# Masked attention sublayers: where VectorE adds the mask to the next scores, and where ScalarE copies the next values

## The chip, the cores and the metric

One NeuronCore of one Trainium2 chip runs the whole program; there is no other core and no collective. The metric is the device time of one execution in microseconds. Before the change it is 3198.39 us, the median of three runs.

## The reference

A decoder of four layers runs on 8 sequences of 100 tokens with 256 features. Each layer is a self-attention, a cross-attention over 361 context rows and a feed-forward part, each on a layer-normed input and added to the stream. Three of the four self-attentions mask their scores, have 16 heads, and are the subject here:

```python
# L0: Q is x itself (16 per head), K = x Wk + bk, V = x Wv + bv (64 per head)
scores = jnp.einsum('bhqd,bhkd->bhqk', Q, K) + mask          # causal
o = jnp.einsum('bhqk,bhkd->bhqd', softmax(scores), V)
return x + gelu(o, approximate=False) @ Wf + bf
# L2: causal, V of 16 per head, no Gelu;  L3: rotary q and k, a window of |i - j| <= 32
```

The fourth (L1) has one head, no mask and a transposed output. The softmax maximum of every query row and head is taken over the masked scores.

## The kernel before, in words

The program has three stages with one instruction stream per engine each (`stream`, written by hand): A, B and C. A stage is a list of items; an item is one sequence of one sublayer. `KINDS` gives the order: A = first (8 items), whole, mixture, turned, cross; B = causal (8), wide; C = band (8), cross. "first" is the masked attention of layer 0 (all heads, with the Gelu), "causal" that of layer 2, "band" that of layer 3. I number the items of each masked sublayer 0 to 7. Between the stages lie feed-forward parts, and behind C a recurrent loop that is most of the time.

An item's step of the loop has four rounds, r = 0 to 3, and in one step of the loop an engine works on several items at once: with item i in the middle, the scores are made for i+1 and the weighted values and the output product for i-1 or i-2. Each engine runs its list strictly in order and waits on semaphores. For the masked kinds the pieces are:

- TensorE makes the scores of item i+1 as rows of queries in PSUM banks 0 to 3 (`score_round`, L748 or L736), in round 0, right after the first of the two key tiles of item i.
- VectorE adds the mask to those rows (L1858, 100 x 1600 elements), waits for itself, and takes the negated maxima (L1860). That is `tops_of`. The maxima free the score banks.
- TensorE turns the maxima (`turn_tops`, L777, at the end of round 3), and VectorE adds them to the queries (`lower`, L1880), so that the second score product comes out with the maximum subtracted.
- TensorE makes the second score product of item i in two key tiles, transposed, in banks 4 and 5 (`key_rows`, L813 or L804), one tile in round 0 and one in round 1. The two tiles use the same banks, so tile 1 waits until ScalarE has taken tile 0.
- VectorE adds the transposed mask to each tile (`mask_rows`, L1888), ScalarE takes its exponential (L1491).
- TensorE multiplies with the values (`weighted_half` L827 and L834 for "first"), VectorE divides by the sum (`divided_half`, last operation L1904; `divided` L1920 for the other kinds), TensorE makes the output product (`out_product`, L905 and L907), VectorE adds it to the stream (`add_out`, L1928).
- For "first", ScalarE takes eight Gelus of 128 x 100 in place (L1590), four per half of the heads, and the output product in round 0 of the next step waits for all eight. TensorE makes the item's own values in two halves (`own_values`, L720, rounds 2 and 3). ScalarE copies half 0 out of PSUM (L1395, round 2), VectorE half 1 (L1979, round 3).
- `group_work` makes what serves four sequences at once: it turns the normed rows (L597) and projects queries and keys (L606), with the copies out of PSUM on ScalarE (L1395) or, for "band", rotations on VectorE (L1829, L1831).

Everything that TensorE writes outside the score and tile banks goes through banks 6 and 7 in turn (`open_m`): a product can start only when the product two before it has been copied out. This ties TensorE's order to ScalarE's and VectorE's order. With item i in the middle, VectorE's order in rounds 0 and 1 for "first" is: output of i-2, division of half 0 of i-1, mask of tile 0, division of half 1, mask of tile 1, mask of the next scores, maxima. For "causal" and "band" there is one division ahead of tile 0 and none between the tiles.

Items with group work in their loop step: first 0, 1, 2 and 6; causal and band 1, 2, 5 and 6. The others I call light.

Of the kernel before, what the change touches and what calls it, by code (L numbers as in the profile page):

```python
# [21 lines left out]
ALU = mybir.AluOpType  # L22
# [128 lines left out]
def build(nc, dram, out):  # L151
    with ExitStack() as ctx:
# [43 lines left out]
        def cst(name):  # L196
            at, n = CONST[name]
            return const[:, at:at + n]
# [243 lines left out]
        def kind_of(ph, i):  # L442

            return KINDS[ph][i // B] if 0 <= i < B * len(KINDS[ph]) else None
# [928 lines left out]
        def _(act):  # L1373
# [103 lines left out]
            def own_values(ph, i, half):  # L1477

                if kind_of(ph, i) == "first":
                    evacuate(mem[ph]["vA"][0:S, i % 2, 512 * half:512 * half + 512], S, 512, ph, "v", i, half)  # L1480
                else:
                    evacuate(v1[0:S, i % 2, 0, :], S, D, ph, "v", i, half)
# [50 lines left out]
            def stream(ph):  # L1533

                nc.scalar.preload_act_table(ACT.Exp)
                for i in range(-3, items_of(ph) + 2):
# [8 lines left out]
                    for r in range(4):  # L1545
# [36 lines left out]
                        if then == "cross" and ph == "C" and r in (1, 2):  # L1582
                            values_of(ph, i + 1, r - 1)
                        group_work(ph, i, r)
                        if past == "first" and r in (1, 2):
                            half = r - 1
                            act.wait_ge(sem["divided"], 2 * (i - 1) + half + 1)
                            for c in range(4 * half, 4 * half + 4):
                                o_ = mem[ph]["oT"][:, columns_of(c)]
                                last = nc.scalar.activation(o_, o_, ACT.Gelu, bias=abv[:, c:c + 1])  # L1590
                            last.then_inc(sem["gelu"], 1)
                        if then in ("first", "turned") and r == 2:
                            own_values(ph, i + 1, 0)
                        if ph == "B":
                            wide_step(ph, i, r, 0)
                            wide_step(ph, i, r, 1)
# [93 lines left out]
        def _(dve):  # L1690
# [142 lines left out]
            def group_work(ph, i, r):  # L1833

                for s, kind in enumerate(KINDS[ph]):
                    for g in range(2):
# [5 lines left out]
                        if kind == "mixture" and (at_, r) == (0, 3):  # L1842
# [5 lines left out]
                            top_two(4, small[:, 0, 0:4, :], small[:, 1, 0:4, :], gates4[:, g, :, 0:E],  # L1848
                                    lambda last: last.then_inc(sem["gates_ready"], 1))

            def tops_of(ph, i, c):

                kind, tops = kind_of(ph, i), mem[ph]["tops"]
                dve.wait_ge(sem["sc_full"], before(ROUNDS, ph, i, c + 1))
                if kind in ("first", "band", "causal"):
                    rows = banks[0:S, 0:4, 0:4 * S].rearrange("p j (c k) -> p j c k", c=4)
                    over = cst("window" if kind == "band" else "causal")[0:S, :].unsqueeze(1).unsqueeze(1).to_broadcast([S, 4, 4, S])
                    step(nc.vector.tensor_tensor(rows, rows, over, ALU.add))  # L1858
                    dst = tops.rearrange("p c (j e) -> p j c e", j=4)[:, :, :, 16]
                    nc.vector.tensor_reduce(dst, rows, AX, ALU.max, negate=True).then_inc(sem["sc_free"], 1)  # L1860
                elif kind == "cross":
                    nc.vector.tensor_reduce(tops[:, c, 16:P:32], banks[0:S, 0:4, 0:NK], AX, ALU.max, negate=True  # L1862
                                            ).then_inc(sem["sc_free"], 1)
                else:
                    keys = NK if kind == "whole" else S
                    nc.vector.tensor_reduce(peak[:, i % 2:i % 2 + 1], banks[0:S, 0, 0:keys], AX, ALU.max, negate=True
                                            ).then_inc(sem["peaks"], 1)
# [142 lines left out]
            def stream(ph):  # L2010

                for i in range(-3, items_of(ph) + 2):
# [6 lines left out]
                    for r in range(4):  # L2019
# [10 lines left out]
                            mask_rows(ph, i, 0)  # L2030
                        if past == "first" and r == 0:
                            divided_half(ph, i - 1, 1)
                        masked_late = now in ("first", "band", "causal") and then in ("first", "band", "causal")
                        if then not in (None, "mixture", "wide") and (r == 0 or then == "cross") and not masked_late:
                            tops_of(ph, i + 1, r)
                        if now in ("first", "band", "causal") and r == 1:
# [1108 lines left out]
```

## Time and profile before

| | |
|---|---|
| median of 3 runs | 3198.39 us (3196.77 to 3203.35) |
| the profiled execution | 3194.56 us |
| its span in the trace | 3192.7 us |
| mean granted TensorE clock | 0.961 of full speed |
| TensorE matmul, VectorE, ScalarE busy | 2961.0, 1556.2, 744.0 us |
| first, causal, band sublayers in the trace | about 29 to 223, 897 to 1009, 1565 to 1684 us |

A time in the timeline is the distance from the span's start. The number in brackets at the end of a row is how long the engine had been idle before that instruction, and what released it. A row without brackets followed directly on the one before. The 2.85 us by which the span is shorter than the execution's own time lie outside the records.

### The profile page before, as it was taken

How to read it: one execution, taken by the hardware profiler on the slowest of the kernel's cores; microseconds unless marked ns; L12 is line 12 of the kernel's file. 1: busy time of each engine (PE TensorE's matmuls, PEld its weight loads, DVE VectorE, ACT ScalarE, POOL GpSimd, SP SyncE). 2: the span in 40 equal slices, each digit the busy share in tenths (PEclk: the TensorE clock that was granted, in tenths of full speed). 3: DMA queues.
4: the chain of work that ended last, by engine and by line, in shares of the span. 5: the costliest groups of instructions: out<-in, count | busy, mean ns of one | idle time of the engine just before them, and what ended most of it. 6: DMA issues, size and time to landing. Idle time of an engine off the chain costs nothing.

```text
span 3192.7 us, 63820 instructions
## 1 busy us (share of the span) xinstructions
PE 2961.0 (93%) x25719; PEld 1664.5 (52%) x25719; DVE 1556.2 (49%) x4141; ACT 744.0 (23%) x1837; POOL 280.7 (9%) x673
## 2 busy tenths in 40 slices
PE   6888889899978999999889999999999999999897
PEld 4554456589755555555546643434444444444386
DVE  4545335411256566300575532466666666666643
ACT  2331123311122455211014411111111111111111
POOL 2112211020311010000311100000000000000011
PEclk9999989999989999999889999999999999999999
DMA  4000000189330000411000156000000000000176
GB/s 148 1 1 1 10 26 15 34 303 326 119 120 1 1 1 1 143 53 66 1 1 3 32 163 176 12 23 24 23 25 20 23 24 24 20 23 24 40 267 228
DMA packets 81363, 202.99 MB, mean 64 GB/s; under 512 B 32894, under 2 KB 56107, under 8 KB 68484
## 3 DMA queue, kind: packets, MB, share of 16 engines
q1 hardware_dynamic: 77208, 192.76, 18.4%
q0 software_dynamic: 3968, 7.56, 0.7%
q8 instruction: 140, 2.29, 0.3%
q14 instruction: 47, 0.39, 0.0%
HBM read 170.06 MB, written 37.53 MB: 65 GB/s over the span
## 4 chain that ended last, share of the span: by engine, by line
PE 79%; DVE 10%; DMA 4%; ACT 3%; issue 2%; POOL 1%; SPq 1%; DVEq 0%; POOLq 0%; ACTq 0%
PE banks L1273 32%; PE banks L1087 7%; PE banks L905 4%; PE banks L606 4%; PE banks L798 2%; PE banks L1151 2%; PE banks L1163 2%; PE banks L927 2%; PE banks L1242 2%; PE banks L559 2%; PE banks L945 1%; PE banks L951 1%; PE banks L967 1%; PE banks L693 1%; PE banks L1320 1%
## 5 line engine op out<-in xcount | busy, mean ns | idle before, releaser
L1273 PE MATMUL banks<-arena 128*32 128x384 f32 x12800 | 1034.3, 486 | 1.9 <-DVE arena L2276 1.1
L1273 PEld LDWEIGHTS banks<-arena 128*32 128x32 f32 x12800 | 416.6, 110 | 613.7 <-issue 610.0
L1663 ACT ACTIVATE arena<-arena 128x256 f32<-128x256 f32 x200 | 83.2, 416 | 759.4 <-DVE arena L2288 759.4
L2288 DVE TENSOR_TENSOR arena<-banks,arena 128x256 f32<-128x256 f32 x200 | 84.9, 425 | 199.8 <-PE banks L1273 198.7
L1087 PE MATMUL banks<-arena 128*128 128x400 f32 x512 | 172.5, 499 | 1.5 <-DVE arena L2239 0.8
L606 PE MATMUL banks<-XNT,arena 128*128 128x400 f32 x384 | 153.2, 542 | 9.7 <-ACT XNT L1395 3.7
L905 PE MATMUL banks<-arena 128*100 128x256 f32 x512 | 139.2, 426 | 14.7 <-ACT arena L1590 5.1
L1384 ACT ACTIVATE arena<-banks 128x512 f32<-128x512 f32 (+2 forms) x103 | 59.2, 575 | 341.8 <-PE banks L1151 137.4
L1087 PEld LDWEIGHTS banks<-arena 128*128 128x128 f32 x512 | 97.1, 190 | 76.8 <-DVE arena L2239 1.4
L1862 DVE TENSOR_REDUCE arena<-banks 100x4 f32<-100x1444 f32 x64 | 106.3, 1661 | 62.8 <-PE banks L754 62.6
L2579 POOL TENSOR_TENSOR rstd<-rstd 100x3 f32<-100x3 f32 (+1 forms) x120 | 23.1, 193 | 1239.5 <-DVE rstd L1817 1233.1
L798 PEld LDWEIGHTS banks<-arena 32*121 32x121 f32 x1536 | 100.6, 187 | 58.5 <-ACT arena L1497 35.7
L1497 ACT ACTIVATE arena<-banks 121x600 f32<-121x600 f32 x128 | 85.8, 670 | 184.4 <-PE banks L798 184.4
L1395 ACT ACTIVATE arena<-banks 128x361 f32<-128x361 f32 (+4 forms) x147 | 72.0, 490 | 233.4 <-PE banks L951 103.0
L2670 POOL DMA_INDIRECT region_rows<-arena x20 | 18.4, 920 | 1226.5 <-DVE arena L2417 1223.4
L905 PEld LDWEIGHTS banks<-arena 128*100 128x100 f32 x512 | 91.7, 186 | 52.2 <-ACT arena L1590 5.9
L798 PE MATMUL banks<-arena 32*121 32x100 f32 x1536 | 112.5, 278 | 6.2 <-ACT arena L1497 6.2
L1087 PE MATMUL banks<-XNT,arena 128*128 128x400 f32 x288 | 101.6, 513 | 11.5 <-DMA arena<-gu 10.5
L606 PEld LDWEIGHTS banks<-XNT,arena 128*128 128x128 f32 x384 | 75.9, 205 | 69.5 <-issue 15.0
L559 PE MATMUL banks<-arena 128*100 128x256 f32 x448 | 100.0, 385 | 5.5 <-DVE X L2162 2.9
L2292 DVE TENSOR_TENSOR arena<-arena,banks 128x128 f32<-128x128 f32 x200 | 57.6, 288 | 96.4 <-ACT arena L1663 96.4
L1928 DVE TENSOR_TENSOR X<-X,banks 100x256 f32<-100x256 f32 x56 | 23.5, 420 | 161.6 <-PE banks L907 101.4
(385 smaller groups left out, 4276.7 us busy)
## 6 DMA issues: line engine op xcount, KB each, us to landing
arena<-fc SPq DMA_DIRECT2D x22, 1024.0 KB, 6.8
arena<-pj SPq DMA_DIRECT2D x22, 1024.0 KB, 5.2
arena<-gu SPq DMA_DIRECT2D x21, 1024.0 KB, 7.1
arena<-whh SPq DMA_DIRECT2D x32, 384.0 KB, 10.8
arena<-dn SPq DMA_DIRECT2D x21, 512.0 KB, 5.3
arena<-xw SPq DMA_DIRECT2D x400, 24.0 KB
xw<-arena SPq DMA_DIRECT2D x6, 1536.0 KB, 7.2
arena<-hh SPq DMA_DIRECT2D x16, 512.0 KB, 3.2
```

The lines of the kernel that those rows point to most:

```text
L559: last = nc.tensor.matmul(u[0:S, 0:cols], a, b, start=i == 0, stop=bias is None and i == len(parts) - 1)
L606: last = nc.tensor.matmul(u[:, 0:4 * S], w[:, kk], XNT[:, kk, columns_of(4 * g, 4)], start=kk == 0, stop=kk == C - 1)
L798: last = nc.tensor.matmul(banks[0:KR, 4 + jj, columns_of(kc)], m["kX"][r, i % 3, c, key_chunk(kc)], qA[r, c, columns_of(b)], start=True, s ...
L905: last = nc.tensor.matmul(u[0:S, 0:D], o_, w_, start=c == 0, stop=bias is None and c == len(parts) - 1)
L927: last = nc.tensor.matmul(u[0:S, 0:cols], XNT[:, kk, columns_of(b)], wa("f_w", C)[:, kk, 512 * j:512 * j + cols], start=kk == 0, stop=j < ...
L1087: last = nc.tensor.matmul(u[:, 0:HALF], w, x[:, half * HALF:(half + 1) * HALF], start=i == 0, stop=i == len(parts) - 1)
L1273: last = nc.tensor.matmul(banks[32 * j:32 * j + 32, 2 * c + i, 0:384].rearrange("p (g n) -> p g n", g=3), hT[:, 1 - i, 32 * ub:32 * ub + 3 ...
L1395: nc.scalar.activation(dst, u[0:rows, 0:cols], func, bias=bias, scale=scale).then_inc(sem[evac_], 1)
L1497: nc.scalar.activation(dst, banks[0:KR, 4:6, 0:KC * S], ACT.Exp).then_inc(sem["t_free"], 1)
L1663: nc.scalar.activation(rz[:, c, :], pre[:, c, :], ACT.Sigmoid).then_inc(sem["rz_done"], 1)
L1862: nc.vector.tensor_reduce(tops[:, c, 16:P:32], banks[0:S, 0:4, 0:NK], AX, ALU.max, negate=True).then_inc(sem["sc_free"], 1)
L2288: nc.vector.tensor_tensor(pre[:, c, :].rearrange("p (g n) -> p g n", g=2), banks[:, 2 * c + i, 0:2 * P].rearrange("p (g n) -> p g n", g=2) ...
```

## The change

It has two parts. On VectorE `tops_of` is cut in two for the masked kinds: the mask on the next scores becomes `mask_scores`, called in round 0 after the mask of key tile 0 (for "first" after the division of half 1 as well), and the maxima stay where they were, behind the mask of tile 1. On ScalarE, for "first", the eight Gelus go together into round 2, and the copy of the next item's value half 0 is put ahead of them. No operation is added or removed.

```diff
                         group_work(ph, i, r)
-                        if past == "first" and r in (1, 2):
-                            half = r - 1
-                            act.wait_ge(sem["divided"], 2 * (i - 1) + half + 1)
-                            for c in range(4 * half, 4 * half + 4):
+                        if then in ("first", "turned") and r == 2:
+                            own_values(ph, i + 1, 0)
+                        if past == "first" and r == 2:
+                            act.wait_ge(sem["divided"], 2 * i)
+                            for c in range(8):
                                 o_ = mem[ph]["oT"][:, columns_of(c)]
                                 last = nc.scalar.activation(o_, o_, ACT.Gelu, bias=abv[:, c:c + 1])
-                            last.then_inc(sem["gelu"], 1)
-                        if then in ("first", "turned") and r == 2:
-                            own_values(ph, i + 1, 0)
+                            last.then_inc(sem["gelu"], 2)
...
+            def mask_scores(ph, i):
+
+                dve.wait_ge(sem["sc_full"], before(ROUNDS, ph, i, 1))
+                rows = banks[0:S, 0:4, 0:4 * S].rearrange("p j (c k) -> p j c k", c=4)
+                over = cst("window" if kind_of(ph, i) == "band" else "causal")[0:S, :].unsqueeze(1).unsqueeze(1).to_broadcast([S, 4, 4, S])
+                step(nc.vector.tensor_tensor(rows, rows, over, ALU.add))
+
             def tops_of(ph, i, c):
 
                 kind, tops = kind_of(ph, i), mem[ph]["tops"]
-                dve.wait_ge(sem["sc_full"], before(ROUNDS, ph, i, c + 1))
+                if kind not in ("first", "band", "causal"):
+                    dve.wait_ge(sem["sc_full"], before(ROUNDS, ph, i, c + 1))
                 if kind in ("first", "band", "causal"):
                     rows = banks[0:S, 0:4, 0:4 * S].rearrange("p j (c k) -> p j c k", c=4)
-                    over = cst("window" if kind == "band" else "causal")[0:S, :].unsqueeze(1).unsqueeze(1).to_broadcast([S, 4, 4, S])
-                    step(nc.vector.tensor_tensor(rows, rows, over, ALU.add))
...
                         if past == "first" and r == 0:
                             divided_half(ph, i - 1, 1)
-                        masked_late = now in ("first", "band", "causal") and then in ("first", "band", "causal")
+                        masked = then in ("first", "band", "causal")
+                        masked_late = now in ("first", "band", "causal") and masked
+                        if masked and r == 0:
+                            mask_scores(ph, i + 1)
                         if then not in (None, "mixture", "wide") and (r == 0 or then == "cross") and not masked_late:
                             tops_of(ph, i + 1, r)
```

## Rows read from the trace of the kernel before

**Rows 1.** The page's chain that ended last, shares by engine.
```profile
PE 79%; DVE 10%; DMA 4%; ACT 3%; issue 2%; POOL 1%; SPq 1%; DVEq 0%; POOLq 0%; ACTq 0%
```
**Rows 2.** Lines L1858, L1860 and L1590: durations in ns (min/median/max), first and last start.
```profile
L1858 DVE TENSOR_TENSOR banks<-banks,const_sb x24: 1822/1823/1833, 29.5 to 1664.9; 100x1600 f32<-100x1600 f32 x24
L1860 DVE TENSOR_REDUCE arena<-banks x24: 1825/1826/1827, 31.4 to 1666.8; 100x16 f32<-100x1600 f32 x24
L1590 ACT ACTIVATE arena<-arena x64: 361/363/378, 61.6 to 218.6; 128x100 f32<-128x100 f32 x64
L1590 ACT ACT_TABLE_LOAD  x8: 1283/1283/1283, 60.3 to 215.0; - x8
```
**Rows 3.** Timeline of first, item 3, rounds 1 to next 0: start us, us, engine, line.
```profile
107.72 0.95 PE L813 MATMUL banks<-arena 32*100 32x100 f32 x16 [0.27 <-ACT arena L1491]
109.07 0.57 DVE L1904 TENSOR_TENSOR arena<-banks,arena 128x400 f32<-128x400 f32 x1
109.68 0.99 DVE L1888 TENSOR_TENSOR banks<-banks,causalT 100x800 f32<-100x800 f32 x1
110.71 0.84 ACT L1491 ACTIVATE arena<-banks 100x800 f32<-100x800 f32 x1 [3.04 <-DVE banks L1888]
111.57 1.28 ACT L1590 ACT_TABLE_LOAD   x1
112.86 2.26 ACT L1590 ACTIVATE arena<-arena 128x100 f32<-128x100 f32 x8
115.02 0.58 ACT L1395 ACTIVATE arena<-banks 100x512 f32<-100x512 f32 x1
115.74 0.53 PE L777 MATMUL banks<-const_sb,arena 100*128 100x100 f32 x4 [2.37 <-ACT arena L1395]
116.11 3.62 PE L905 MATMUL banks<-arena 128*100 128x256 f32 x16
```
**Rows 4.** Timeline of first, item 1, rounds 2 and 3.
```profile
66.62 0.60 ACT L1395 ACTIVATE arena<-banks 100x512 f32<-100x512 f32 x1
69.11 1.88 PE L720 MATMUL banks<-arena,XNT 128*100 128x512 f32 x4
70.83 0.51 PE L777 MATMUL banks<-const_sb,arena 100*128 100x100 f32 x4
```
**Rows 5.** Timeline of first, item 6, rounds 2 and 3.
```profile
174.86 0.60 ACT L1395 ACTIVATE arena<-banks 100x512 f32<-100x512 f32 x1
177.72 0.51 PE L777 MATMUL banks<-const_sb,arena 100*128 100x100 f32 x4
```
**Rows 6.** Timeline of first, item 7: the second key product, the output product.
```profile
193.59 0.87 PE L693 MATMUL banks<-arena 128*128 128x361 f32 x2 [1.06 <-ACT arena L1395]
197.60 6.60 PE L905 MATMUL banks<-arena 128*100 128x256 f32 x16 [2.71 <-ACT arena L1590]
```
**Rows 7.** Timeline of causal, item 3, rounds 0 to 2.
```profile
944.53 0.99 DVE L1888 TENSOR_TENSOR banks<-banks,causalT 100x800 f32<-100x800 f32 x1
947.33 3.49 PE L905 MATMUL banks<-arena 128*100 128x256 f32 x8
947.44 1.00 DVE L1888 TENSOR_TENSOR banks<-banks,causalT 100x800 f32<-100x800 f32 x1 [1.92 <-PE banks L813]
950.21 1.83 DVE L1860 TENSOR_REDUCE arena<-banks 100x16 f32<-100x1600 f32 x1
951.95 0.41 DVE L1928 TENSOR_TENSOR X<-X,banks 100x256 f32<-100x256 f32 x1
```
**Rows 8.** Timeline of band, items 3 and 4: TensorE.
```profile
1625.59 1.97 PE L905 MATMUL banks<-arena 128*100 128x256 f32 x8
1630.35 0.93 PE L777 MATMUL banks<-const_sb,arena 100*128 100x100 f32 x4 [2.79 <-DVE arena L1860]
1638.40 3.74 PE L905 MATMUL banks<-arena 128*100 128x256 f32 x8
```
**Rows 9.** Windows: length; PE, PEld, DVE, ACT, POOL busy (count); granted clock; DMA.
```profile
1632.00:1645.00 13.00, 10.85 (x68) 5.41 (x60) 9.61 (x16) 1.67 (x2) 6.13 (x16) 0.50 0.01 2
```

## The prediction

> **What bounds the kernel now.** I read the chain of waits first: TensorE holds 79% of it and VectorE 10% [rows 1]. The recurrent loop and the feed-forward parts make up most of the TensorE share, and the change doesn't touch them. Then I read the timeline of the three masked sublayers, since a sum over the program says nothing about an edit of order. There no engine is full: TensorE, VectorE and ScalarE hand work to each other, and one item's loop step is as long as the longest ring of waits. So the question for each of the items is which instruction ends the ring, and whether the moved work stands ahead of it.
>
> The moved VectorE instruction takes 1.82 us and stands 24 times in the program; three of these (ahead of item 0 of each sublayer, where nothing masked is in the middle) keep their place, so 21 move [rows 2]. One place on VectorE costs 1.86 us, the 1.82 and a short wait for itself. Its maxima (1.83 us) stay.
>
> **Part one, causal and band (14 moves).** Between the masks of the two key tiles VectorE idles: 1.92 us with TensorE at full clock [rows 7], since the exponential and the second tile must come between. The next scores are ready by then, as TensorE makes them right behind tile 0. The moved mask starts 0.9 us after the start of the tile 0 mask (that is how closely masks follow one another) and is through 2.77 us after it; the tile 1 mask starts 2.91 us after it now (947.44 less 944.53). It fits, with 0.14 us to spare, and with more where the clock is half. So the maxima come 1.86 us sooner in all 14, and what that is worth depends on what comes next:
> - Where only the maxima are waited for, all 1.86 us. In band item 3 TensorE's turning of the maxima sat idle for 2.79 us behind them, and its output product had ended long before, at 1627.56 [rows 8]. Causal item 0 and band items 0 and 3 are so: 3 x 1.86 = 5.6.
> - Where the output product ends shortly before the maxima, the gain stops there. In causal item 3 VectorE adds the output at 951.95, right behind the maxima, but the product ends at 947.33 + 3.49 = 950.82 [rows 7]: 1.95 less 0.88, so 1.07. I work causal 4 and band 4 (its L905 ran 3.74 us from 1638.40 [rows 8]) in the same way: 0.82 and 0.83. Sum 2.7.
> - In band item 2 the rotations stand between the tiles. The mask goes in front of them and pushes the tile 1 mask 0.97 us back, and the maxima gain the rest, 0.88. In causal 2 and 6 TensorE is nearly full with projections and waited only 0.38 us on this: 0.8 for both. Sum 1.6.
> - In causal 1 and 5 and band 1, 5 and 6 the copy of the turned rows or TensorE's own work ends the ring: 0.
> The bounds: no gain at all, and 14 x 1.86 = 26. I take 5.6 + 2.7 + 1.6 = 9.9 us gained.
>
> **Part two, first (7 moves, and all the Gelus).** Here VectorE isn't idle between the tiles, because the division of half 1 stands there. In item 3 its last operation starts at 109.07 and the tile 1 mask follows at 109.68 without a wait, though TensorE had that tile ready at 107.72 + 0.95 = 108.67 [rows 3]. So the moved mask pushes the tile 1 mask, and ScalarE's exponential behind it, back by 1.86 us, while the maxima end where they did. Queued behind that exponential on ScalarE are the copies of round 1, the table load and the Gelus.
> - Light items 3, 4, 5. Now: exponential 110.71, table load, eight Gelus to 115.12, value copy 115.02, then the turning of the maxima at 115.74 (it waited 2.37 us for the copy's bank), then the output product at 116.11 [rows 3]. After: exponential 112.57, copy 113.30 to 113.90, load 1.29, Gelus 2.26 to 117.45, output product 117.5. The turning moves forward to 114.35, but the output product is ahead of everything of the next round 0 in TensorE's queue and now waits for the Gelus. Loss 1.4 each, 4.1 for three. The stall behind the copy goes; the Gelus are late next.
> - Item 1. The value copy stood at 66.62 [rows 4]; after: 68.48 to 69.08. Four Gelus used to be behind the exponential and four between copies; now load 1.28 and eight Gelus (2.26) follow and end at 72.6, and the copy of the third key projection (0.60) only then frees the bank for value half 1. That product starts at 73.2 instead of 69.11, and the turning, 1.72 us behind it, at 74.9 instead of 70.83 [rows 4]. Loss 4.1.
> - Item 6 has the same order with a query projection: 174.86 + 1.86 + 0.60 + 1.28 + 2.26 + 0.60 = 181.5 for the turning instead of 177.72 [rows 5]; the output product used to start 1.0 us behind it and now 0.4. Loss 3.1.
> - Item 2. TensorE reaches tile 1 late there and the moved mask is covered, but a query copy falls behind the Gelus: 0.3.
> - Items 7 and 8 (8 is the step in which the last Gelus are taken). No mask moves. The first four Gelus and the load ran while TensorE made the keys; now the load starts only behind the second key copy, whose product ends at 193.59 + 0.87 = 194.46: 194.46 + 0.58 + 1.28 + 2.26 = 198.6, while now the last Gelu ends and the output product starts at 197.60 [rows 6]. Loss 1.0 each, 2.0.
> - Item 0: TensorE is full, 0.
> Bounds: 8 us if TensorE's own stream hides half of items 1 and 6, 25 us if each lengthened gap also costs clock (below). I take 4.1 + 4.1 + 3.1 + 0.3 + 2.0 = 13.6 us lost. The table loads stay at 8 [rows 2].
>
> **Sum.** 13.6 - 9.9 = +3.7 us. Against the profiled execution, 3194.56 (span 3192.7 and 1.9 around it), that is 3198.3. That execution is 3.8 below the median of the runs, 3198.39, so I forecast 3202.1 for the median.
>
> **The clock.** TensorE's output product of 16 matmul passes took 3.62 us in item 3 and 6.60 in item 7 behind a 2.71 us gap [rows 3, 6], so a gap of this size can leave it at 1.2 GHz for 2.98 us more; the 2.37 us gap in item 3 did not. After the change the gap ahead of that product is 2.6 us in the light items. The Trainium skill ("TensorE: Matmul & The Clock Gate", section "Why this matters for your kernels") asks that no long idle gaps stand between bursts, because the array falls back to half clock; it speaks against the change in "first" and for it in causal and band. Item 7 agrees with it; item 3 shows that its gap was still short enough.
>
> **The rivals.**
> - Clock lost in first (chance 0.25). Three of the seven lengthened gaps (items 1 and 3 to 8) leave the output product at half clock: 3 x 2.98 = 8.9, so 3202.1 + 8.9 = 3211. For it: item 7. Against it: item 3 at a gap 0.3 us shorter.
> - Clock won in causal and band, the other side (0.15). In band item 4 the granted clock was 0.50, that is 1.2 GHz [rows 9]. Its output product, now what ends the ring, takes 3.74 us against 1.97 in item 3 [rows 8], and the turning 0.93 against 0.51 [rows 4, 8]. The tile 1 product takes 0.7 more as well, by the 2.63 us that VectorE idled ahead of some tile 1 masks against the 1.92 of [rows 7]. If shorter gaps keep the clock at 2.4 GHz, that is 2.9 per item. It decides from four such items on: 11.6, so 3202.1 - 11.6 = 3190.5. Against it: VectorE and ScalarE still take most of the ring, so gaps remain.
> - The moves don't count (0.10). The causal and band gains and the first losses are both taken up by what stands next in TensorE's order: 3198. For it: heavy items give 0 already.
> - My sum as it stands: 0.50.
>
> **How the numbers follow.** A measurement of this kernel can tell about 0.2% (6.4 us) from no change, so "same" is 3192.0 to 3204.8. The forecast case lies in it with about three quarters of its weight, since 2.7 us more are enough to leave it (0.38 same, 0.12 slower); the third rival lies in it wholly, and 0.02 of each clock case. Slower: 0.12 + 0.23 = 0.35. Faster: 0.13. Same: 0.38 + 0.10 + 0.04 = 0.52. The range: 3192 to 3212 leaves out most of the second rival and little of the first.
>
> **What would show it.** In the changed profile: in causal and band the next scores' mask starts 0.9 us behind the tile 0 mask, the tile 1 mask keeps its 2.9 us distance, and causal and band are 4.5 and 5.4 us shorter. In first the idle ahead of the tile 1 mask is nil and its distance from the division 1.86 us larger; the turning of the maxima waits for them and no longer for the copy; the output product waits for the Gelus; the step of items 3 to 5 grows from 18.4 to 19.8 us, and the last Gelu comes 12 to 14 us later. I am wrong if the light items of first don't grow, if the tile 1 mask of causal slips by more than 0.2 us, or if the clock in rows like [rows 9] moves by tenths.

## The result, and the profile after

The changed kernel took 3213.9 us in the median of 5 executions (3202.66 to 3223.18) against 3201.47 for the kernel before on the same chip (3196.77 to 3203.48): a ratio of 1.0042, 95% interval 1.0025 to 1.006. Timed once more on another chip it was 1.0056 (1.0027 to 1.0085). So the change makes the kernel slower by 12 to 15 us. I had forecast 3202.1, with 3192 to 3212 as the range: the sign of the sum was right, the time lay 1.9 us above the range, and "same", to which I had given the most weight (0.52), was not it.

The profiled execution of the changed kernel took 3204.47 us (span 3202.7), and its span is 10.0 us longer than that of before. (Time less span is 1.8 us here and was 1.9 before, 3194.56 less 3192.7; the 2.85 us given ahead of the prediction is wrong.) The windows say where. First the kernel before; the columns are those of [rows 9]; the stretches are the all-head first sublayer, the expert part of layer 1, causal, band, and the stretch behind band.

```profile
33.30:223.20 189.90, 149.22 (x1187) 94.15 (x1187) 94.81 (x180) 67.10 (x129) 20.02 (x51) 0.91 0.02 9
650.30:706.10 55.80, 54.89 (x332) 46.59 (x331) 7.12 (x22) 8.67 (x14) 16.38 (x18) 1.00 0.72 263
896.70:1009.50 112.80, 91.42 (x891) 63.48 (x888) 69.72 (x99) 23.25 (x36) 9.46 (x28) 0.80 0.09 30
1570.20:1686.20 116.00, 93.14 (x552) 50.66 (x553) 77.57 (x107) 20.60 (x33) 9.45 (x28) 0.74 0.00 1
...
1686.20:2000.10 313.90, 293.31 (x2670) 164.61 (x2672) 123.46 (x217) 91.02 (x160) 18.91 (x56) 0.98 0.33 95
```

The same matmuls of the first four in the changed kernel:

```profile
33.30:243.60 210.30, 157.91 (x1187) 98.57 (x1187) 94.86 (x180) 67.30 (x129) 19.88 (x51) 0.86 0.02 8
667.30:732.70 65.40, 57.34 (x332) 48.06 (x331) 6.93 (x22) 8.69 (x14) 16.39 (x18) 0.95 0.61 223
921.80:1027.20 105.40, 88.33 (x893) 61.87 (x890) 69.52 (x99) 23.26 (x36) 9.46 (x28) 0.83 0.09 32
1587.90:1694.20 106.30, 85.58 (x552) 46.54 (x553) 77.41 (x107) 20.63 (x33) 9.45 (x28) 0.82 0.00 1
```

VectorE and ScalarE are busy for the same time in each pair; what moves is the length and the granted clock. I use one more quantity below: half-clock time, (1 - granted clock) x 2 x length, which is the time that TensorE spent at 1.2 GHz if the rest was at 2.4. In first it goes from 189.9 x 0.09 x 2 = 34 us to 210.3 x 0.14 x 2 = 59.

One execution doesn't do here. Lengths in us by stretch, cut at the same matmuls, in five profiled executions (`before`, `before_again`, `after`, `after_again`, `after_timed`; a few tenths lie between these cuts and the windows above):

| stretch | before | before, again | after | after, again | after, third |
|---|---|---|---|---|---|
| first (touched) | 190.0 | 189.8 | 210.4 | 210.7 | 210.5 |
| first to layer 1's experts | 427.0 | 427.0 | 423.7 | 423.9 | 423.7 |
| experts of layer 1 | 55.8 | 55.6 | 65.4 | 55.7 | 55.6 |
| causal (touched) | 112.9 | 112.5 | 105.4 | 109.1 | 108.8 |
| causal to band | 560.7 | 560.7 | 560.7 | 564.8 | 564.8 |
| band (touched) | 116.0 | 115.9 | 106.3 | 107.2 | 108.5 |
| 314 us behind band | 313.9 | 313.7 | 315.6 | 339.2 | 320.3 |
| span | 3192.7 | 3189.9 | 3202.7 | 3227.0 | 3206.7 |

First costs 20.4 to 20.9 us each time, where I forecast 13.6. Causal gives back 3.5 to 7.5 (forecast 4.5), band 7.4 to 9.7 (5.4). Together the touched stretches cost 3.2 to 9.6 us. The rest is in stretches without a changed instruction, the one behind band above all: up to 25 us. From first to the experts it is 3.1 to 3.3 us shorter in all three traces, from causal to band 4.1 longer in two.

**The rings of waits are as forecast, in item 3.** Item 3 of first in the changed kernel, the rows that answer to [rows 3]:

```profile
115.47 0.57 DVE L1909 TENSOR_TENSOR arena<-banks,arena 128x400 f32<-128x400 f32 x1
116.08 1.83 DVE L1855 TENSOR_TENSOR banks<-banks,const_sb 100x1600 f32<-100x1600 f32 x1
117.95 1.00 DVE L1893 TENSOR_TENSOR banks<-banks,causalT 100x800 f32<-100x800 f32 x1
118.98 0.84 ACT L1491 ACTIVATE arena<-banks 100x800 f32<-100x800 f32 x1 [4.91 <-DVE banks L1893]
119.71 0.59 ACT L1395 ACTIVATE arena<-banks 100x512 f32<-100x512 f32 x1
120.32 1.28 ACT L1591 ACT_TABLE_LOAD   x1
120.72 0.56 PE L777 MATMUL banks<-const_sb,arena 100*128 100x100 f32 x4 [0.95 <-DVE arena L1865]
121.62 2.26 ACT L1591 ACTIVATE arena<-arena 128x100 f32<-128x100 f32 x8
123.92 5.38 PE L905 MATMUL banks<-arena 128*100 128x256 f32 x16 [2.64 <-ACT arena L1591]
```

Division, moved mask (L1855), tile 1 mask (L1893), exponential, value copy, load, Gelus, output product: each stands where the forecast put it. From the division to the tile 1 mask it is 2.48 us, against 0.61 before: the 1.86. The turning (L777) waits for the maxima, the output product for the Gelus. What I had not put into the sum is its length, 5.38 us where [rows 3] has 3.62: 1.76 more, at half clock in this execution. The chain of waits over this stretch, in order of time (start, us, what), shows that all of it is on the path:

```profile
116.08 1.84 DVE banks L1855
117.95 1.01 DVE banks L1893
118.98 0.84 ACT arena L1491
119.81 0.49 ACT arena L1395
120.32 1.28 ACT L1591
121.62 2.27 ACT arena L1591 x8
123.92 5.38 PE banks L905 x16
```

The same product in items 4, 5, 7 and 8 of the changed kernel, from TensorE's timeline. In the kernel before these four took 3.62, 4.89, 6.60 and 3.70 us, so items 4 and 8 are slower now, and items 5 and 7 are not:

```profile
145.48 5.34 PE L905 MATMUL banks<-arena 128*100 128x256 f32 x16 [2.11 <-ACT arena L1591]
...
167.20 3.67 PE L905 MATMUL banks<-arena 128*100 128x256 f32 x16 [2.40 <-ACT arena L1591]
...
215.50 6.16 PE L905 MATMUL banks<-arena 128*100 128x256 f32 x16 [3.79 <-ACT arena L1591]
...
237.91 5.21 PE L905 MATMUL banks<-arena 128*100 128x256 f32 x16 [3.79 <-ACT arena L1591]
```

Which of these products falls into half clock differs between executions of the same kernel. In `after_timed` item 3's ran at full clock, 3.70 us, and the value product two ahead of it (L720) at half, 5.37 us for 3.68 in `after`; the step was as long, 19.81 us:

```profile
117.90 5.37 PE L720 MATMUL banks<-arena,XNT 128*100 128x512 f32 x8 [1.02 <-DVE arena L1909]
...
125.73 3.70 PE L905 MATMUL banks<-arena 128*100 128x256 f32 x16 [2.11 <-ACT arena L1591]
```

In `after_again` it was item 4's that ran at full clock (3.70 us). Item 8's was slow in all three (5.21, 5.38 and 5.26 us).

In item 1 the first projection (L606) took 5.44 us for 4.54 before, and the second value product (L720) behind the Gelus 3.62 us where [rows 4] has 1.88:

```profile
61.88 5.44 PE L606 MATMUL banks<-XNT,arena 128*128 128x400 f32 x8 [3.59 <-ACT XNT L1395]
69.07 0.60 ACT L1395 ACTIVATE arena<-banks 100x512 f32<-100x512 f32 x1 [1.12 <-PE banks L720]
73.77 3.62 PE L720 MATMUL banks<-arena,XNT 128*100 128x512 f32 x4 [2.05 <-ACT arena L1395]
77.23 0.51 PE L777 MATMUL banks<-const_sb,arena 100*128 100x100 f32 x4
```

In causal the moved mask (L1855) fits between the two tiles' masks, which answers to [rows 7]:

```profile
967.60 0.99 DVE L1893 TENSOR_TENSOR banks<-banks,causalT 100x800 f32<-100x800 f32 x1
968.50 1.82 DVE L1855 TENSOR_TENSOR banks<-banks,const_sb 100x1600 f32<-100x1600 f32 x1
970.58 1.00 DVE L1893 TENSOR_TENSOR banks<-banks,causalT 100x800 f32<-100x800 f32 x1 [0.26 <-PE banks L813]
971.49 1.81 DVE L1865 TENSOR_REDUCE arena<-banks 100x16 f32<-100x1600 f32 x1
```

The moved mask starts 0.90 us behind the tile 0 mask, and the tile 1 mask waits 0.26 us for TensorE, not for VectorE. The forecast of 0.9 us holds, and the tile 1 mask stands 2.98 us behind the tile 0 mask instead of 2.91, so it is pushed by 0.07.

In band items 3 and 4, which answer to [rows 8], the turning of the maxima no longer waits 2.79 us, and the output product of item 4 is back at 1.97 us from 3.74. That is so in this execution; in `after_again` and `after_timed` it took 3.73 and 3.74 us:

```profile
1639.46 2.79 PE L905 MATMUL banks<-arena 128*100 128x256 f32 x8
1642.43 0.93 PE L777 MATMUL banks<-const_sb,arena 100*128 100x100 f32 x4 [0.18 <-DVE arena L1865]
1649.34 1.97 PE L905 MATMUL banks<-arena 128*100 128x256 f32 x8
```

### The profile page after: what moved, and what is told of

It is laid out like the page before. It is cut to its first block, busy times and chain, and to the rows that moved or that the text cites. A ratio compares the mean times of both kernels' runs of the same rounds, so it can differ in the third digit from the quotient of the medians.

```text
span 3202.7 us, 63841 instructions
## 1 busy us (share of the span) xinstructions
PE 2956.7 (92%) x25719; PEld 1660.6 (52%) x25719; DVE 1554.6 (49%) x4141; ACT 744.2 (23%) x1837; POOL 281.3 (9%) x673
## 4 chain that ended last, share of the span: by engine, by line
PE 80%; DVE 9%; ACT 4%; DMA 3%; issue 2%; POOL 1%; SPq 1%; another core or an unknown queue 0%; DVEq 0%; POOLq 0%; ACTq 0%
PE banks L1273 32%; PE banks L1087 8%; PE banks L905 4%; PE banks L606 4%; PE banks L798 2%; PE banks L559 2%; PE banks L1151 2%; PE banks L1163 2%; PE banks L927 2%; PE banks L1242 2%; PE banks L945 1%; PE banks L951 1%; PE banks L693 1%; PE banks L967 1%; PE banks L754 1%
## 5 line engine op out<-in xcount | busy, mean ns | idle before, releaser
L606 PE MATMUL banks<-XNT,arena 128*128 128x400 f32 x384 | 150.9, 535 | 11.2 <-ACT XNT L1395 5.6
L1867 DVE TENSOR_REDUCE arena<-banks 100x4 f32<-100x1444 f32 x64 | 106.3, 1660 | 62.6 <-PE banks L754 62.4
L1087 PE MATMUL banks<-XNT,arena 128*128 128x400 f32 x288 | 101.8, 514 | 11.6 <-DMA arena<-gu 10.6
L606 PEld LDWEIGHTS banks<-XNT,arena 128*128 128x128 f32 x384 | 74.3, 202 | 70.0 <-issue 13.1
```

The lines of the kernel that those rows point to most:

```text
L606: last = nc.tensor.matmul(u[:, 0:4 * S], w[:, kk], XNT[:, kk, columns_of(4 * g, 4)], start=kk == 0, stop=kk == C - 1)
L1087: last = nc.tensor.matmul(u[:, 0:HALF], w, x[:, half * HALF:(half + 1) * HALF], start=i == 0, stop=i == len(parts) - 1)
```

## The experiments

**1. Each part alone.** `scalar_only` is the kernel before with the Gelu part (value copy ahead of one run of eight Gelus). `vector_first` moves the mask in first alone, `vector_layers23` in causal and band alone. The last two differ from each other in one line:

```
- late = then != "first" and masked_late     # vector_first
+ late = then == "first" and masked_late     # vector_layers23
  if masked and r == 0 and not late:
      mask_scores(ph, i + 1)                 # early, ahead of tile 1's mask
  ...
  if late:
      mask_scores(ph, i + 1)                 # where it stood before
```

> Only ScalarE's part of the change (value copy ahead, eight Gelus together in round 2); VectorE as before. Theory (the output product waits for the Gelus): light items of first gain 0.35 us each (copy no longer behind the Gelus), item 1 loses 2.3, item 6 1.3, item 2 0.3, items 7 and 8 1.0 each: sum +4.8 us, and up to 4 us more by half-clock phases. Nothing changes in causal and band. Rival (this part is what the words of the change suggest, a stall removed): every item of first shortens by 0.4 us or more, sum -3 us or better.

> Only VectorE's early mask, and in the first sublayer alone; causal, band and ScalarE as before. Theory: the mask stands ahead of the tile 1 mask without cover in items 1, 3, 4, 5 and 6, 1.86 us each, and is covered in items 0 and 2: +9.3 us, plus clock. The tile 1 mask has no idle time ahead of it in the light items. Rival (VectorE's order costs nothing, the loss of the whole change is the Gelus' alone): within 2 us of before.

> VectorE's early mask in causal and band alone; first and ScalarE as before. Theory: -9.9 us by the ring lengths; the trace of the changed kernel shows 7.5 us in causal and 8.6 in band, since shorter gaps also spare half-clock phases: -10 to -16 us, ratio about 0.996. Rival (the gain is taken up by TensorE's order or given back by clock later): 0 to -4 us.

Measured beside before at 3203.04: `scalar_only` 3205.41, ratio 1.0 (0.9985 to 1.0015); `vector_first` 3215.25, 1.0037 (1.0014 to 1.006); `vector_layers23` 3199.01, 0.9979 (0.9955 to 1.0002). The slowdown comes from the mask moved in first, and in the trace of `vector_first` the first sublayer is 19.6 us longer than before, nearly all that the whole change costs there:

```profile
32.00:241.60 209.60, 157.75 (x1187) 99.86 (x1187) 94.99 (x181) 67.13 (x129) 21.55 (x53) 0.85 0.03 11
```

My sum for it was 9.3 us plus clock, and the half-clock time is 209.6 x 0.15 x 2 = 63 us against 34. In `vector_layers23` causal and band were 17.2 us shorter, above the 10 to 16 expected, but the time gained less than that. The item step of first that has no half-clock time in any of the kernels (items 2 to 3, from output product to output product) took 18.45 us before, 18.20 in `scalar_only`, 20.32 in `vector_first` and 19.81 in the changed kernel: the 1.87 of the mask, less what the value copy brings when it no longer stands behind the Gelus, gives the forecast 1.4 (1.36). The copy brings 0.25 us of this without the mask and 0.51 beside it. In its trace `scalar_only` has 201.8 us for first, 11.8 more than before, half-clock time 48 against 34 us, though its median is the same. I had 4.8 us for it, and up to 4 by clock. The stretch from first to the experts gives 5.2 us back (421.8 for 427.0), so in the trace it nets 6.6; the rest I can't bring together with the median from one trace. The losses of the parts in first don't add up either: 11.8 and 19.6 us alone, 20.4 to 20.9 together.

**2. Keep TensorE busy in the lengthened gaps.** `after_fill` is the changed kernel with nine added products (18 matmul passes) behind the turning of the maxima in items 3, 4, 5, 7 and 8 of first. They write columns that nobody reads.

```
+ if ph == "A" and r == 3 and i in (3, 4, 5, 7, 8):
+     for _ in range(9):
+         nc.tensor.matmul(banks[0:S, 3, 4 * S:512], ident[:, 0:S], ident[:, 0:112],
+                          start=True, stop=True, skip_group_check=True)
```

> The changed kernel with nine added TensorE products of 112 columns, into columns that nobody reads, behind the turning of the maxima in items 3, 4, 5, 7 and 8 of first: they fill the gap in which TensorE waits for the Gelus. Clock theory: no wait gets shorter, but the output products of items 3, 4, 7 and 8, which took 5.1 to 6.1 us in the changed kernel, take 3.6: -5 to -7 us against the changed kernel, and the granted clock of the stretch rises from 0.86. Rival (the slow products are not due to the gap ahead of them): the products cost 0 to +5 us, and nothing is gained.

Measured: 3206.14, ratio 1.0011 (0.9992 to 1.0029), where the changed kernel has 1.0042 and 1.0056, each beside the kernel before on a chip of its own. Items 3 and 8 in its trace (TensorE; compare the products at 123.92 and 237.91 above):

```profile
123.30 1.89 PE L1064 MATMUL banks<-const_sb 128*100 128x112 f32 x18
125.58 3.70 PE L905 MATMUL banks<-arena 128*100 128x256 f32 x16 [0.39 <-ACT arena L1595]
...
235.21 3.70 PE L905 MATMUL banks<-arena 128*100 128x256 f32 x16 [2.06 <-ACT arena L1595]
```

Both products take 3.70 us. For item 3 this proves nothing: `after_timed` has 3.70 there, and the same 5.37 us of L720 ahead of it, without an added product. Item 8's is the one that was slow in all three traces of the changed kernel. Item 7's still took 5.38 us, behind the added work. The steps that end in items 4, 5 and 7 took 19.87, 20.03 and 19.87 us without half-clock time, against 21.55, 21.72 and 21.17 in `after` (19.86, 21.77 and 21.16 in `after_timed`); first as a whole 206.0 against 210.4 to 210.7 in all three. That adding work takes time away shows that these 4.4 us, of which 3.5 lie in items 7 and 8, are clock and not waits. I had expected 5 to 7 us. And 19.87 less the 18.38 of before is 1.5, again the forecast 1.4; for item 7, 19.87 less 18.84 is the forecast 1.0.

**3. The gain without the loss.** `layers23_again` is `vector_layers23` on another chip. `copy_and_fill` adds to it the value copy between the two halves of the Gelus in first items 3 to 5, and added products into unread columns: nine in first items 7 and 8, six of 96 columns each ahead of the turning of the maxima in causal and band items 1, 4 and 5.

```
  if past == "first" and r in (1, 2):
      half = r - 1
+     if r == 2 and i in (3, 4, 5):
+         own_values(ph, i + 1, 0)
      act.wait_ge(sem["divided"], 2 * (i - 1) + half + 1)
...
+ if ph in "BC" and i in (1, 4, 5):
+     for _ in range(6):
+         nc.tensor.matmul(u[0:S, 416:512], ident[:, 0:S], ident[:, 0:96], ...)
  wait("sc_free", before(ROUNDS, ph, i + 1))
```

> The kernel before once more, for a second trace. Its runs spread over 30 us, and in each kernel the slower runs show a lower granted clock. Clock theory: the three masked sublayers and the stretch of the first expert part differ from the first trace by half-clock phases only, some 5 to 15 us in all, in stretches that no edit touched; the expert part, 55.8 us in the first trace of this kernel and 61.7 to 65.4 in all others, is again above 60. Rival (the first trace is typical): every stretch within 2 us of the first trace.

> VectorE's early mask in causal and band alone, once more, for a second trace and more rounds: the first had a ratio of 0.9979 though causal and band were 17.2 us shorter in its trace. Theory (the rings are 10 us shorter, the rest is clock that comes and goes): causal and band together 10 to 17 us shorter again, ratio 0.995 to 0.998. Rival (the 17.2 us were one lucky execution, and the edit gives nothing): a ratio of 0.999 or more and causal and band within 4 us of before.

> The candidate to beat both: early mask in causal and band alone; ScalarE's value copy between the two halves of the Gelus in items 3, 4 and 5 of first alone; and added TensorE products into unread columns where it waits (six ahead of the turning of the maxima in the light items of causal and band, nine ahead of the output product in items 7 and 8 of first). Theory: -10 us by the shorter rings, -1 by the copy, -3 to -8 by fewer half-clock phases than before: ratio 0.993 to 0.996, and the half-clock time in causal and band under 60 us (104 before, 78 with the early mask alone). Rival (added products only delay): no better than 0.998.

> The changed kernel once more, for a second trace. Theory: first is 13.6 us longer than before by the rings and 3 to 10 more by half-clock phases, causal and band together 10 to 18 us shorter, and what else differs from before lies in the expert part and is not the change's. Rival (the expert part is slow because of the change): it is above 65 us here and under 60 in the second trace of before.

`copy_and_fill` had 3186.04, ratio 0.996 (0.994 to 0.9981), at the edge of what I expected, with 70 us of half clock in causal and band where I wanted under 60. `layers23_again` had a median of 3188.14, beside 3196.5 of before, but a ratio of 1.0 (0.9971 to 1.003), not 0.995 to 0.998: seven of its twelve executions lay at 3178 to 3190 us and five at 3208 to 3216. The means are 3195.4 against 3196.6 us (without one of before at 3551.85), and with two groups the median says little. The single profiled executions of before and of the changed kernel took 3191.7 and 3228.87. For before my theory was wrong and the rival right: all stretches of the table lie within 1 us of the first trace, the experts at 55.6. The second was 20.7 us longer in first and 12.6 shorter in causal and band, as expected, but the experts were at 55.7, and it opened the question of the stretch behind band, 339.2 us there. In these windows (the first 80 us behind band, then the rest) it ran at a clock of 0.83 and 0.92:

```profile
1695.80:1775.80 80.00, 76.18 (x705) 50.34 (x704) 34.51 (x47) 29.52 (x50) 9.47 (x28) 0.83 0.00 1
1775.80:2034.90 259.10, 242.85 (x1963) 130.64 (x1965) 88.46 (x170) 61.45 (x111) 9.46 (x28) 0.92 0.40 115
```

**4. Does the copy or do the added products bring it?** `copy_between` is `copy_and_fill` without the added products.

> The changed kernel as it is, timed once more beside the kernel before. Rings and their clock (my theory): the rings cost +3.7 us net; with the clock time that the traces showed in the first sublayers (about 7 more lost) and in causal and band (about 6 won) the three masked stretches give +3 to +5 us, and what the executions showed over that (12 us in the medians) was spread of the untouched stretches. Median 3 to 8 us above the kernel before, ratio 1.001 to 1.0025. Rival, the change also brings the half-clock stretches in the expert part and the last cross sublayer: again 10 us or more above, ratio 1.003 to 1.006.

> The kernel before with the early mask in causal and band alone, and in items 3, 4 and 5 of the first sublayer the value copy between the two halves of the Gelus (they keep their halves). No filling products. Ring theory: the copy stands where the bank is wanted and no Gelu is late, so the first items 3 to 5 get 0 to 0.5 us each shorter and causal and band stay at 105 to 107 us each; 3 times 0.3 from the version without the copy: ratio 0.994 to 0.998, as copy_and_fill. Rival, the filling products carried the gain of copy_and_fill (0.996): ratio 0.998 to 1.0 and 40 us or more of half clock in causal and band against 30 to 39 there.

> copy_and_fill once more, on the same chip as copy_between: with filling products into unread columns. If the filling holds the clock up by itself, its mean is 3 us or more below copy_between's; if not, within 3 us of it.

Little of this went as my theory had it. `after_timed` was 3211.47, ratio 1.0056 (1.0027 to 1.0085), not 1.001 to 1.0025; the rival had the size, but not the place, since the experts took 55.6 us in its trace. `copy_between` had one execution at 3178.63 and five at 3204 to 3211: median 3207.49, 1.0039 (1.0026 to 1.0052), though the mean of all six, 3202.96, is only 1.002 times that of before, 3196.58. `copy_fill_timed` had 3193.47, 0.9983 (0.9964 to 1.0002), so 0.996 does not repeat on this chip, but 11 of its 12 lay below 3202, and its mean is 11.6 us below that of `copy_between`, as the theory on filling had it (3 us or more). The copy itself did its part: the steps that end in items 3 to 5 took 17.98, 18.28 and 18.13 us against 18.45, 18.38 and 18.66. What the five long executions were, its one profile, of the 3178.63, doesn't show.

**5. Profiles of the long executions.** Two more of each kernel.

> copy_between, one more profiled execution. If it is a long one (3204 us or more): by my theory causal, band and the first sublayer keep the lengths of its first profile (105, 107, 189 us) and the untouched stretch behind band is 339 us in place of 314, at half clock. Rival: causal and band are back at 110 us or more each.

> The early mask in causal and band alone, one more profiled execution. As copy_between_look1: a long one shows the stretch behind band at 339 us (theory), or causal and band longer (rival); a short one (about 3180) says nothing new.

> copy_between, a third profiled execution; as copy_between_look1.

> The early mask in causal and band alone, a further profiled execution; as layers23_look1.

Three were long: 3208.49, 3204.86 and 3209.81; `layers23_look2` was 3172.65. In all three long ones the stretch behind band is 339.1 to 339.3 us, in the short ones 314.1. `copy_between`, short:

```profile
1666.70:1980.90 314.20, 293.57 (x2667) 164.15 (x2669) 122.88 (x217) 91.05 (x160) 19.02 (x56) 0.98 0.33 95
```

`copy_between_look1`, long: the whole stretch, and 10 us of it.

```profile
1675.60:2014.80 339.20, 319.03 (x2670) 180.90 (x2672) 122.78 (x217) 91.02 (x160) 18.91 (x56) 0.90 0.31 88
...
1690.00:1700.00 10.00, 10.00 (x53) 6.76 (x52) 1.66 (x1) 3.50 (x6) 0.00 (x0) 0.50 0.00 0
```

Equal work, 25.0 us longer, 339.2 x 0.10 x 2 = 68 us of half clock against about 13. Within the long stretch TensorE is busy for all of 1690 to 1700 and still at 1.2 GHz. The same holds for all 17.0 us from 1686.2 to 1703.2. My part of the expectation on causal was off: both further traces of `copy_between` have 108.9 us there, not 105, and then the stretch from causal to band is 564.8 in place of 560.7. `layers23_look1` has 105.3 and 560.7 and is long all the same.

**6. Which place of the edit brings it.** The early mask in causal alone, in band alone, and in causal with the copy of `copy_between`:

```
- late = then == "first" and masked_late
+ late = then in ("first", "band") and masked_late      # causal_only, copy_causal
+ late = then in ("first", "causal") and masked_late    # band_only
```

> The kernel before with the early mask in the causal sublayer alone. Theory (the long executions come from band's shorter steps, which let the stretch behind band start at half clock): executions lie together, no group 25 us or more above the lowest, median 3 to 8 us below the kernel before (causal 105 to 109 us in place of 112.9), ratio 0.9975 to 0.999; the stretch behind band stays at 314 us. Rival (any shift of the clock's phase does it, the causal edit too): a quarter or more of the executions 20 us above the lowest.

> The kernel before with the early mask in band alone. Theory: two groups of executions, one 9 us below the kernel before and one 15 to 17 us above it (25 us for the stretch behind band, less 9), a quarter to three quarters in the upper one; ratio 0.998 to 1.004. Rival: one group, 5 to 9 us below the kernel before, ratio 0.997 to 0.9985.

> copy_between with the early mask in causal alone, band and the first sublayers' masks as before; the value copy between the Gelu halves in first items 3 to 5. Theory: as causal_only and up to 1 us less, ratio 0.997 to 0.999, without copy_between's upper group (5 of 6 executions at 3204 to 3211). Rival: the copy brings that group, so it is here too.

Beside before at 3198.72 (29 executions): `causal_only` 3188.88, all 12 in 3185 to 3198, ratio 0.9976 (0.9964 to 0.9989). `copy_causal` 3193.46, all 12 in 3183 to 3202, 0.9984 (0.997 to 0.9998). `band_only` has five executions at 3184 to 3190 and six at 3210 to 3215 (a twelfth, 5025 us, is far from all others and left out of this), ratio 1.0012 (0.9987 to 1.0037). `causal_only` gained 9.8 us where I expected 3 to 8. `copy_causal`, for which I expected up to 1 us less than that, is 4.6 above it, so the copy shows no gain in the time. The windows of `causal_only` (causal, band, behind band) and of `band_only` (band):

```profile
897.40:1002.80 105.40, 87.24 (x891) 60.88 (x890) 69.42 (x100) 23.34 (x36) 9.45 (x28) 0.84 0.10 34
1563.50:1679.40 115.90, 93.03 (x552) 50.62 (x553) 77.62 (x107) 20.64 (x33) 9.45 (x28) 0.74 0.00 1
...
1679.40:1993.30 313.90, 293.37 (x2670) 164.68 (x2672) 123.41 (x217) 91.03 (x161) 18.90 (x56) 0.98 0.33 95
```

```profile
1567.80:1673.90 106.10, 85.45 (x551) 46.60 (x552) 77.34 (x107) 20.58 (x32) 9.45 (x28) 0.82 0.00 1
```

So band's edit alone brings the second group; causal's alone, and causal's with the copy, do not. The one trace of `band_only` is of its fastest execution, with 315.6 us behind band; that its upper group is the 339 us stretch is inferred from the distance of the groups. `causal_only` beats the kernel before by an interval that leaves out 1, and the changed kernel was slower than before wherever it was timed.

## Why the prediction was wrong

**The forecast gains and losses in waits: right in the main.** The mask in causal fits (0.90 us behind, the tile 1 mask pushed by 0.07). Where the granted clock is the same in both kernels, the item steps changed as worked out: causal item 0 -1.80 (forecast 1.86), band item 0 -1.80, band item 2 -0.92 (0.88), causal items 2 and 6 -0.56 and -0.65 (0.8 for both, so 1.2 measured), light items of first +1.36, and +1.5 for the others with the clock held by added work. In item 6 I forecast 3.1 and it was 1.5: the output product that opens its step took 4.89 us before and 3.67 after, 1.2 us that I had not looked at. In item 1 it was 6.4 for my 4.1. (My sums also lose up to 0.1 us each to rounding: three light items make 4.2, the gains 10.0.)

**The step that failed: "I take 4.1 + 4.1 + 3.1 + 0.3 + 2.0 = 13.6 us lost", with the clock kept out of the sum.** First lost 20.4 to 20.9. The excess of 6.8 to 7.3 is clock in the main: 25 us more at 1.2 GHz in the first trace. There it lies in the output products of items 3, 4 and 8 (5.38, 5.34 and 5.21 us, 1.5 to 1.8 more than before each), in item 1 (L606 and L720, 2.3 us above my forecast for the item) and in the step that ends in item 7 (2.3 longer for my 1.0). Item 7's product is none of it: 6.16 us, and 6.60 before. Item 6 takes 1.6 off. Of the 6.8, `after_fill` took 4.4 away again; for the rest the reading is by the half-clock time alone. The profile had told me that such a gap can cost 2.98 us [rows 6], and I had named the price of three such items, 8.9 us, as a rival at 0.25. It belonged into the sum, at some weight: every gap ahead of the output product in the light items was to become 2.6 us, beside the 2.71 of [rows 6]. My argument against it, that 2.37 us had been short enough in item 3, compared gaps alone, and the gap doesn't decide (last section). The rule of the Trainium skill that I cited ("TensorE: Matmul & The Clock Gate", section "Why this matters for your kernels") spoke against the change in first. The traces bear out its direction, with some 25 to 31 us more at half clock in first; they also show half clock behind gaps as short as 2.11 us.

**The same term the other way.** Causal gained 3.5 to 7.5 and band 7.4 to 9.7, against 4.5 and 5.4. The step of band that ends in item 4 went from 12.82 us to 9.83 in the first trace, 3.0 where I had 0.83, and its half-clock time from 12.8 us to nothing, as the second rival had it; in the other two traces it took 11.38 and 11.67 us. Both clock rivals came true in part: the first had 8.9 us and it was about 7, the second 11.6 and it was 3.6 in the mean. In the touched stretches they nearly cancel: +20.6 - 4.9 - 8.6 = +7.1 us in the mean of the three traces, and my sum was +3.7. That the measured 3213.9 lies close to the 3211 of the first rival is luck: what it describes is partly cancelled, and the rest came from elsewhere. Two of the signs that I had named also came out against me: the clock in the rows of band moved by tenths, and the last Gelu came 18.9 us later, not 12 to 14.

**The other term at nothing.** The words "and the change doesn't touch them", said of the loop and the feed-forward parts, put all stretches without a changed instruction at 0. With the early mask in band, the stretch behind it is 25 us longer in some executions: 4 of 14 traces of such versions had 339 us, the other ten 314 to 321; six of six traces of versions without it had 313.7 to 314.1. In the times this is the upper group of `copy_between` and `layers23_again` (three long executions of these two kernels were traced), by inference that of `band_only`, and probably most of the changed kernel's executions from 3218 up, of which the one of 3228.87 was traced. In the mean of its three traces this stretch costs 11 us, more than the touched ones together. By these traces this was the larger miss, and enough to carry the time out of my range; a sum over the changed instructions can't find it. Its size is uncertain: the three traces are 20.8 us above the two of before in the mean, the timings 12 to 15. And 3.1 of the 11.8 us between 3202.1 and 3213.9 are not the change's at all: before had 3198.39 in three executions and 3201.47 in five.

**What stays open.** What decides in an execution between 314 and 339 us is not shown. Band took 107.16 to 107.21 us in the four long traces and in no other, so the state in which band ends may matter to tenths of a microsecond; that was seen afterwards and not tested. Of the 24 timed executions of `copy_and_fill` none was above 3203.1, while five of six of `copy_between` were, on the same chip as half of the 24; so the added products may keep the long stretch away, but which of them, and how, was not run. The 65.4 us of layer 1's experts in one trace of the changed kernel (55.6 and 55.7 in the others) is not explained either. It does not follow the edit: the four traces taken on one chip (`scalar_only`, `vector_first`, `vector_layers23`, `after_fill`) have 61.7 to 65.1 us, the 14 from four other chips 55.6 to 56.3, of the same kernels in part. Nor is the +11.8 in the trace of `scalar_only`.

## What to carry to other kernels

Where TensorE sits idle in every step, an edit of order shifts the phases in which it runs at half clock: take the price of one from the profile (here 1.5 to 3 us for one output product) and put it into the sum, for each gap that grows and each that shrinks. Then look at the stretch behind the edit too, and read several executions: one trace of a kernel whose times lie in two groups shows one of the two. When the places of an edit share one mechanism, time each alone: here the mask in causal is a gain of 0.24%, in band none that can be measured, and in first the loss. And before an added or moved instruction gets the credit for a product that became fast, look for the same product in a second trace of the kernel without it.

## What the runs showed of the hardware

- The gap ahead of a product did not decide its clock: in `after` it ran at full clock behind 2.40 us (3.67 us) and at half behind 2.11 us (5.34 us), and in `after_timed` at full behind 2.11 us (3.70 us).
- A full stream does not bring the clock back at once: 17.0 us with TensorE busy throughout (`copy_between_look1`, 1686.2 to 1703.2) stood at 0.50.
- Added products that compute nothing made a stretch shorter: with 18 passes (1.89 us in item 3) in each of five steps, first took 206.0 us, and 210.4 to 210.7 without them.
- A load of the Gelu's table took 1.28 us, and the first Gelu started 1.30 us after the load's start, so nothing came on top there.
